# One exp for both units of a head in the last attention, and two smaller edits elsewhere, in an eight-stage decoder kernel

## The chip, the cores and the metric

The kernel runs on one core of a Trainium2 chip. The metric is the device time of one execution in microseconds. The kernel before was timed three times: 2863.63 us is the median, 2861.47 and 2869.18 us the lowest and highest.

## What is computed

The reference sends a residual stream `x` of 16 tiles of 128 rows by 256 columns through four pairs of a cross attention and a feed-forward part, each added to `x`. The change touches three of the eight stages. The stage that matters most is the last attention: 2048 queries against 2048 keys, 16 heads of 16 columns, with quantised queries, keys, values and weights.

```python
def _L3_xattn_ref(x, cond, Wq, bq, Wkv, bkv, Wp, bp):
    q = (x @ Wq + bq).reshape(1, B * N, H, hd)
    ...
    q = _fq_sym(q, axis=-1)
    k = _fq_sym(k, axis=-1)
    v = _fq_sym(v, axis=2)
    attn = jnp.einsum('bhqd,bhkd->bhqk', q, k)
    attn = jax.nn.softmax(attn.astype(jnp.float32), axis=-1)
    attn = _fq_unsigned(attn, axis=-1)
    out = jnp.einsum('bhqk,bhkd->bhqd', attn, v)
```

The second is the attention of the first feed-forward slot (`gqa`: 16 query heads and 4 key heads of 128 columns, softmax over 128 keys with a causal mask), the third the masked cross attention with the ternary feed-forward part (`mask_bit`).

## The kernel before, in words

Every stage is one block in which each engine has its own instruction list, written out by hand; semaphores tie the lists together. An engine runs its list strictly in order, so an instruction that waits holds back all that stand behind it.

**Last attention (`attend3`).** The work is cut into 512 units. A unit `u` is one tile of 128 query rows (`t = u // 32`), one head and one half of the keys: 128 x 1024 scores. Two units make a head, 32 units a tile. A unit passes through these steps:

1. `score(u)` on TensorE: two matmuls of 512 columns into one of three two-bank slots `S[:, u % 3]` of PSUM (6 of the 8 banks).
2. `maximum(u)` on VectorE: scales the scores, writes them to `kept[:, u % 4]` in SBUF and takes the row maximum. The odd unit goes on from the maximum of the even one.
3. `bias(n)` on GpSimd, once for each head: turns the maximum into exp's bias.
4. `exp(u)` on ScalarE: 128 x 1024, writes the counts `ex[:, u % 4]` as uint16 and sums them.
5. `turn(u)` on TensorE: eight transposes into the one bank `TPW`.
6. `evacuate(u)`: copies the turned bank to `pw[:, u % 4]`, on ScalarE for three units of four, on VectorE for the fourth.
7. `attend(u)` on TensorE: eight matmuls of 16 columns with the values.

TensorE's list is `score(u)`, `turn(u - 4)`, `attend(u - 5)`. At each tile's end VectorE adds up and inverts the sums (`row_steps`), and scales the output (`scale_rows`, `scale_columns`).

**Grouped attention (`gqa`).** The loop over 16 tiles is pipelined: in step `i` TensorE turns and scores tile `i`, then does the queries and values of tile `i + 2`, then `turn_p(i)`, `attend(i)`, `project(i)`. In the last two steps (`i` = 14 and 15) there is no tile `i + 2`. `exp(t)` has four groups of four heads; `sums(t)` on VectorE waits for all four, inverts the 16 sums and multiplies 128 x 2048 at once; `turn_p(t)` waits for that, turns four groups of four heads, and `turned_p(t)` copies them on ScalarE.

**Masked attention (`mask_bit`).** Eight pairs of tiles. TensorE's step `i` begins with `scores(i)`, right behind the `turn_x(i)` that ends step `i - 1` and that ScalarE copies (`turned_x`) before the scores can begin. `keep_busy(nc, k, bank, n)` issues `n` matmuls of 512 columns whose results nobody reads; there is one such call in each step, before `turn_b`.

Of the kernel before, what the change touches and what calls it, by code (L numbers as in the profile page):

```python
# [16 lines left out]
P = 128  # L17
# [663 lines left out]
def gqa(nc, k, x_in, hid_out, arena, load_next, hand):  # L681
# [8 lines left out]
    with ExitStack() as ctx:  # L690
# [116 lines left out]
        def _(act):  # L807
# [29 lines left out]
            def exp(t):  # L837
                for b in range(4):
# [5 lines left out]
            def turned_p(t):  # L844
                for g in range(PG):
# [9 lines left out]
            for i in range(-2, B):  # L855
# [4 lines left out]
                at(exp, i)  # L860
                at(queries, i + 2)
                at(values, i + 2)
                at(turned_p, i)
# [3 lines left out]
        def _(dve):  # L867
# [68 lines left out]
            def sums(t):  # L936
                dve.wait_ge(s["exped"], t * 4 + 4)
                nc.vector.reciprocal(mx[:, 2], mx[:, 1]).then_inc(s["row_recip"], 1)
                dve.wait_ge(s["row_recip"], t + 1)
                nc.vector.tensor_tensor(pr[:], pr[:], mx[:, 2].unsqueeze(2).to_broadcast([P, GH, P]), ALU.mult).then_inc(s["p_norm"], 1)  # L940
# [17 lines left out]
        def _(pe):  # L958
# [1629 lines left out]
def attend3(nc, k, qT_in, steps, out, KT, V, v_step, load_next, hand, qt):  # L2588
# [8 lines left out]
    LAG = 4  # L2597
    LN255 = 5.541263545158426
    with ExitStack() as ctx:
        def sb(name, shape, dt=F32):  # L2600
# [4 lines left out]
            zeroed scores kept bias exped turned evacuated  # L2605
            attended both row_recip probs_step scaled o_done""")
# [7 lines left out]
        sums = sb("sums", [P, 2, 2, NH])  # L2614
        tot = sb("tot", [P, 2, 3, NH])
# [5 lines left out]
        block = ctx.enter_context(nc.Block())  # L2621

# [121 lines left out]
        def _(pe):  # L2744
# [33 lines left out]
            for u in range(NU + LAG + 1):  # L2778
                if u < NU:
                    score(u)  # L2780
# [630 lines left out]
```

## Time and profile before

| | |
|---|---|
| median of three runs | 2863.63 us |
| the profiled execution, its own time | 2859.6 us |
| its span, first to last instruction | 2857.8 us |
| mean granted TensorE clock | 0.964 |
| busy: TensorE, VectorE, ScalarE, GpSimd | 85%, 67%, 59%, 20% |
| last attention | about 1660 to 2498 us of the span |
| grouped attention | about 190 to 697 us |
| masked attention | about 970 to 1150 us |

The shares of busy time are means over stages with different limits: what a stage is bound by has to be read inside it. A duration in the timeline runs from an instruction's start to its end, and the next one often starts some 0.1 us before that end, so what an instruction costs its engine is the distance between two starts.

### The profile page before, as it was taken

What the parts mean: (1) busy time and instruction counts of PE and PEld (TensorE: products, weight loads), DVE (VectorE), ACT (ScalarE), POOL (GpSimd) and SP (SyncE); (2) the same over time, 40 slices, a digit from 0 to 9 for tenths busy, and PEclk for the clock granted to TensorE, in tenths of its full rate; (3) what the DMA queues carried; (4) which work ended last, traced back from release to release, by engine and by line L of the source; (5) the groups of instructions that cost most, each with busy time, mean ns of one, the idle gap of its engine ahead of it and who ended that gap; (6) DMA issues with size and microseconds to landing.
All of it is one profiled execution on the core that took longest, in us unless ns stands there. A gap on an engine that the chain in (4) does not pass through costs nothing. (4 is left out here: it accounts for less than half of the span.)

```text
span 2857.8 us, 52551 instructions
## 1 busy us (share of the span) xinstructions
PE 2421.5 (85%) x19942; PEld 1626.7 (57%) x19942; DVE 1910.8 (67%) x4532; ACT 1689.4 (59%) x3423; POOL 581.8 (20%) x658
## 2 busy tenths in 40 slices
PE   6978999997999786788897777777777777799999
PEld 5745766665666543566565544444444444456666
DVE  6856666663344288675776889999999999833231
ACT  4536676764333266344443489999999999823222
POOL 2214434340221133321221310000000000021211
PEclk9989999999999889999999999999999999999999
DMA  3120000002010210211002220000000000000000
GB/s 142 41 82 8 8 12 16 8 5 80 15 34 8 77 57 15 77 38 43 21 25 85 89 100 16 9 15 11 9 24 9 9 17 9 7 24 23 19 4 12
DMA packets 58953, 92.93 MB, mean 33 GB/s; under 512 B 5440, under 2 KB 54608, under 8 KB 57680
## 3 DMA queue, kind: packets, MB, share of 16 engines
q1 hardware_dynamic: 58704, 89.57, 9.4%
q8 instruction: 161, 2.64, 0.4%
q14 instruction: 88, 0.72, 0.1%
HBM read 66.48 MB, written 23.07 MB: 31 GB/s over the span
## 5 line engine op out<-in xcount | busy, mean ns | idle before, releaser
L2671 ACT ACTIVATE attend_ex<-attend_kept,attend_mx 128x1024 uint16<-128x1024 f32 x512 | 588.1, 1153 | 2.6 <-POOL attend_mx L2656 2.6
L2764 PEld LDWEIGHTS psum<-ident_b,attend_ex 128*128 128x128 bf16 x4096 | 241.7, 98 | 424.2 <-ACT attend_ex L2671 332.1
L2764 PE MATMUL psum<-ident_b,attend_ex 128*128 128x128 bf16 x4096 | 316.5, 221 | 186.2 <-ACT attend_pw L2676 87.9
L2697 DVE CUSTOM_DVE_ANT_0 attend_kept<-psum,attend_zero,attend_mx 128x1024 f32<-128x1024 f32 x256 | 343.8, 1343 | 65.4 <-PE psum L2755 62.3
L1502 PE MATMUL psum<-arena,moe_tokT 128*128 128x512 f32 (+2 forms) x896 | 359.4, 546 | 3.0 <-DVE moe_h L1389 2.9
L2697 DVE CUSTOM_DVE_ANT_0 attend_kept<-psum,attend_zero,queries_step 128x1024 f32<-128x1024 f32 x256 | 327.5, 1279 | 11.9 <-PE psum L2755 9.3
L2755 PE MATMUL psum<-keys_turned,queries_ahead 96*128 96x512 bf16 x1024 | 308.2, 383 | 3.1 <-PEq L2271 2.0
L2676 ACT COPY attend_pw<-psum 128x512 f32<-128x512 f32 x384 | 222.6, 580 | 51.7 <-PE psum L2764 51.5
L1389 DVE TENSOR_TENSOR moe_h<-moe_sg,psum 128x512 f32<-128x512 f32 (+1 forms) x112 | 69.9, 625 | 263.9 <-PE psum L1502 256.7
L1502 PEld LDWEIGHTS psum<-arena,moe_tokT 128*128 128x128 f32 x896 | 165.2, 191 | 138.3 <-issue 119.3
L1236 ACT ACTIVATE moe_sg<-psum 128x512 f32<-128x512 f32 (+1 forms) x112 | 61.4, 548 | 290.3 <-PE psum L1502 286.0
L2656 POOL TENSOR_SCALAR attend_mx<-attend_mx 128x1 f32<-128x1 f32 x256 | 50.8, 199 | 779.0 <-DVE attend_mx L2697 779.0
L2774 PE MATMUL psum<-values,attend_pw 128*128 128x16 f16 x4096 | 178.9, 170 | 3.5 <-DVE stored_rows L2719 2.9
L1524 PE MATMUL psum<-arena,moe_hT 128*128 128x256 f32 (+1 forms) x800 | 178.9, 380 | 2.7 <-ACT moe_hT L1248 1.6
L1194 POOL TENSOR_TENSOR moe_h<-moe_h,moe_cw 128x1408 f32<-128x1408 f32 (+1 forms) x32 | 90.6, 2832 | 374.6 <-DVE moe_h L1389 367.3
L1524 PEld LDWEIGHTS psum<-arena,moe_hT 128*128 128x128 f32 (+1 forms) x800 | 150.8, 190 | 28.2 <-issue 3.3
L2774 PEld LDWEIGHTS psum<-values,attend_pw 128*128 128x128 f16 x4096 | 157.4, 97 | 5.8 <-issue 5.1
L793 POOL TENSOR_TENSOR gqa_nq<-gqa_nq,neg_half 128x20 f32<-128x20 f32 x16 | 88.2, 5511 | 148.5 <-DVE gqa_nq L911 148.5
L1246 ACT COPY moe_hT<-psum 128x512 f32<-128x512 f32 (+1 forms) x112 | 54.1, 527 | 108.7 <-PE psum L1514 108.7
L989 PE MATMUL psum<-arena,gqa_hT 128*128 128x512 f32 x256 | 113.6, 597 | 0.0
L1039 PE MATMUL psum<-arena,gqa_oT 128*128 128x256 f32 x512 | 113.1, 379 | 0.0
L1039 PEld LDWEIGHTS psum<-arena,gqa_oT 128*128 128x128 f32 x512 | 97.3, 190 | 20.1 <-issue 7.7
(454 smaller groups left out, 4732.3 us busy)
## 6 DMA issues: line engine op xcount, KB each, us to landing
residual<-stored_rows SPq DMA_DIRECT2D x48, 128.0 KB, 1.7
queries_turned<-queries_rows SPq DMA_DIRECT2D x16, 384.0 KB, 3.2
queries_ahead<-queries_turned SPq DMA_DIRECT2D x16, 384.0 KB, 3.3
arena<-in_moe SPq DMA_DIRECT2D x1, 5704.0 KB, 18.1
arena<-in_gqa SPq DMA_DIRECT2D x1, 5440.0 KB, 17.8
arena<-in_moe SPq DMA_DIRECT2D x1, 4360.0 KB, 13.2
xatt_ct<-in_ctx_T SPq DMA_DIRECT2D x32, 128.0 KB, 2.2
residual<-stored_rows SPq DMA_DIRECT2D x16, 256.0 KB, 2.1
```

Of the source, the lines that this page charges most:

```text
L793: nc.gpsimd.tensor_tensor(nq[:, j, 1], nq[:, j, 0], k["neg_half"][:].to_broadcast([P, HQK]), ALU.pow).then_inc(s["q_rms"], 1)
L989: last = nc.tensor.matmul(BIG[:, b], hT[:, ic], wq[:, ic, b * 512:(b + 1) * 512], start=ic == 0, stop=ic == DC - 1)
L1039: last = nc.tensor.matmul(Y, oT[:, c], wo[:, c], start=c == 0, stop=c == GH - 1)
L1194: nc.gpsimd.tensor_tensor(hv, hv, cw[:, i % 2, j].unsqueeze(2).to_broadcast([P, SETS, I]), ALU.mult).then_inc(s["h_done"], 1)
L1502: last = nc.tensor.matmul(bank[:, q % 2, 0:size], tokT[:, i % 2, j, ic], wt[:, ic, at:at + size], start=ic == 0, stop=ic == DC - 1)
L1524: last = nc.tensor.matmul(YB[:, j * D:(j + 1) * D], hT[0:size, j, c], wd[0:size, c], start=c == 0, stop=c == DN - 1)
L2671: nc.scalar.activation(ex[:, u % 4], kept[:, u % 4], ACT.Exp, bias=mx[:, t % 2, h, 2:3], accum_out=sums[:, t % 2, u % 2, h:h + 1]).then_in ...
L2676: nc.scalar.copy(pw[:, u % 4], TPW).then_inc(s["evacuated"], 1)
L2697: nc.vector.tensor_tensor_reduce(kept[:, u % 4], S[:, u % 3], zero[:].to_broadcast([P, UK]), steps[:, 0, t, h:h + 1], best[:, 0:1] if half ...
L2755: last = nc.tensor.matmul(S[:, u % 3, b * 512:(b + 1) * 512], qt[:, t % 2, h * P:(h + 1) * P], KT[:, c:c + 4, h // 2], start=True, stop=True)
L2764: last = nc.tensor.transpose(TP[:, c], counts[u % 4][:, c * P:(c + 1) * P], k["ident_b"][:])
L2774: last = nc.tensor.matmul(O[:, h * HD:(h + 1) * HD], pT[u % 4][:, c], V[:, kc, h * HD:(h + 1) * HD], start=kc == 0, stop=kc == B - 1)
```

## The change

Three edits.

In `attend3` the two exps of a head become one over 128 x 2048. To keep both units of a head next to each other for longer, `kept` has eight slots instead of four and moves into the weight arena that the stage does not use. The scores have two PSUM slots instead of three, and the two banks set free give the turned counts three banks instead of one. ScalarE copies 15 of 16 turned banks, VectorE the sixteenth (before 3 of 4 and 1 of 4). TensorE issues five units of scores first, and then `turn(u)`, `score(u + 5)`, `attend(u - 2)`. The two partial sums are one, so that an add in `row_steps` goes.

In `gqa` VectorE normalises each group of four heads as soon as its exps are done, and TensorE turns it on its own. In the last two tiles ScalarE puts the first group's copy ahead of the fourth group's exps.

In `mask_bit` four filler matmuls stand ahead of the scores of pairs 1 to 7.

```diff
 # attend3
-        S = k["psum"][:, 0:6, :].rearrange("p (u b) c -> p u (b c)", b=2)
-        TPW = k["psum"][:, 6, :]
-        TP = TPW.bitcast(BF16).rearrange("p (c m) -> p c m", m=P)
+        S = k["psum"][:, 0:4, :].rearrange("p (u b) c -> p u (b c)", b=2)
+        TPW = k["psum"][:, 4:7, :]
+        TP = TPW.rearrange("p r c -> p (r c)").bitcast(BF16).rearrange("p (r c m) -> p r c m", r=TR, m=P)
-        kept = sb("kept", [P, 4, UK])
+        kept = arena[:, 0:KR * UK].rearrange("p (r c) -> p r c", r=KR)
...
+        def on_dve(u):
+            return u % DR == DR - 1
...
-            def exp(u):
-                t, h = u // UN, u % UN // 2
-                if u % 2 == 0:
-                    act.wait_ge(s["bias"], u // 2 + 1)
-                if u >= 4:
-                    act.wait_ge(s["turned"], u - 3)
-                nc.scalar.activation(ex[:, u % 4], kept[:, u % 4], ACT.Exp, bias=mx[:, t % 2, h, 2:3],
-                                     accum_out=sums[:, t % 2, u % 2, h:h + 1]).then_inc(s["exped"], 1)
+            def exp(n):
+                t, h, u = n // NH, n % NH, 2 * n
+                act.wait_ge(s["bias"], n + 1)
+                if n >= 2:
+                    act.wait_ge(s["turned"], u - 2)
+                nc.scalar.activation(ex[:, u % 4:u % 4 + 2], kept[:, u % KR:u % KR + 2], ACT.Exp, bias=mx[:, t % 2, h, 2:3],
+                                     accum_out=sums[:, t % 2, h:h + 1]).then_inc(s["exped"], 2)
...
-            for u in range(0, NU, 2):
-                exp(u)
-                if u % 4 == 2:
-                    evacuate(u - 1)
-                exp(u + 1)
-                evacuate(u)
+            for n in range(NU // 2 + 1):
+                if n < NU // 2:
+                    exp(n)
+                for u in range(2 * n - 2, 2 * n):
+                    if u >= 0 and not on_dve(u):
+                        evacuate(u)
...
-                if u >= 4:
-                    dve.wait_ge(s["exped"], u - 3)
+                if u >= KR:
+                    dve.wait_ge(s["exped"], u - KR + 1)
...
-            for u in range(NU + LAG + 1):
+            for u in range(5):
+                score(u)
+            for u in range(NU + 2):
                 if u < NU:
-                    score(u)
-                if LAG <= u < NU + LAG:
-                    turn(u - LAG)
-                if u > LAG:
-                    attend(u - LAG - 1)
+                    turn(u)
+                if u + 5 < NU:
+                    score(u + 5)
+                if u >= 2:
+                    attend(u - 2)
 # gqa: ScalarE, VectorE, TensorE
+                else:
+                    exp(i, range(0, 3))
+                    turned_p(i, range(0, 1))
+                    exp(i, range(3, 4))
+                    turned_p(i, range(1, PG))
...
-                dve.wait_ge(s["exped"], t * 4 + 4)
-                nc.vector.reciprocal(mx[:, 2], mx[:, 1]).then_inc(s["row_recip"], 1)
+                for b in range(4):
+                    heads = slice(4 * b, 4 * b + 4)
+                    dve.wait_ge(s["exped"], t * 4 + b + 1)
...
-                pe.wait_ge(s["p_norm"], t + 1)
                 for g in range(PG):
                     n = t * GROUPS + QG + g
+                    pe.wait_ge(s["p_norm"], t * 4 + g + 1)
 # mask_bit, TensorE
             for i in range(NI + 2):
+                if 1 <= i < NI:
+                    keep_busy(nc, k, 6, 4)
                 at(scores, i)
```

On ScalarE in the last attention, before, from inside the first tile: `attend_ex<-attend_kept` is an exp, `attend_pw<-psum` the copy of a turned bank.

```order
L2676 COPY attend_pw<-psum 128x512
L2671 ACTIVATE attend_ex,attend_sums<-attend_kept,attend_mx 128x1024
L2676 COPY attend_pw<-psum 128x512
L2671 ACTIVATE attend_ex,attend_sums<-attend_kept,attend_mx 128x1024
L2676 COPY attend_pw<-psum 128x512
L2671 ACTIVATE attend_ex,attend_sums<-attend_kept,attend_mx 128x1024 x2
```

And now, around the first turned bank that VectorE takes (`arena` is where `kept` lies):

```order
L2690 COPY attend_pw<-psum 128x512 x2
L2685 ACTIVATE attend_ex,attend_sums<-arena,attend_mx 128x2048
L2690 COPY attend_pw<-psum 128x512 x2
L2685 ACTIVATE attend_ex,attend_sums<-arena,attend_mx 128x2048
L2690 COPY attend_pw<-psum 128x512
L2685 ACTIVATE attend_ex,attend_sums<-arena,attend_mx 128x2048
L2690 COPY attend_pw<-psum 128x512 x2
```

Each exp covers a head; two copies stand between two exps, or one.

On TensorE, from the start of the same stage, before: `ident_b` marks the turning, `values` the attending, `keys_turned` the scoring.

```order
L2755 MATMUL psum<-keys_turned,queries_ahead 128x512 x10
L2764 MATMUL psum<-ident_b,attend_ex 128x128 x8
L2755 MATMUL psum<-keys_turned,queries_ahead 128x512 x2
L2764 MATMUL psum<-ident_b,attend_ex 128x128 x8
L2774 MATMUL psum<-values,attend_pw 128x16 x8
L2755 MATMUL psum<-keys_turned,queries_ahead 128x512 x2
L2764 MATMUL psum<-ident_b,attend_ex 128x128 x8
L2774 MATMUL psum<-values,attend_pw 128x16 x8
```

And now:

```order
L2767 MATMUL psum<-keys_turned,queries_ahead 128x512 x10
L2776 MATMUL psum<-ident_b,attend_ex 128x128 x8
L2767 MATMUL psum<-keys_turned,queries_ahead 128x512 x2
L2776 MATMUL psum<-ident_b,attend_ex 128x128 x8
L2767 MATMUL psum<-keys_turned,queries_ahead 128x512 x2
L2776 MATMUL psum<-ident_b,attend_ex 128x128 x8
L2767 MATMUL psum<-keys_turned,queries_ahead 128x512 x2
L2786 MATMUL psum<-values,attend_pw 128x16 x8
L2776 MATMUL psum<-ident_b,attend_ex 128x128 x8
L2767 MATMUL psum<-keys_turned,queries_ahead 128x512 x2
```

In the steady part the scores now stand behind the turning and are for a unit five ahead, and the attending is for a unit two behind; there are as many matmuls as before.

On ScalarE at the end of the grouped attention, before: `gqa_pr` is an exp (16 heads), `gqa_pT` the copy of a turned group, `gqa_oT` a copy of the attended heads.

```order
L848 COPY gqa_pT<-psum 128x512 x4
L853 COPY gqa_oT<-psum 128x512 x4
L835 COPY gqa_qkT<-psum 128x512 x5
L841 ACTIVATE gqa_pr,gqa_mx<-gqa_pr,gqa_mx 128x128 x16
L848 COPY gqa_pT<-psum 128x512 x4
L853 COPY gqa_oT<-psum 128x512 x4
```

And now, in the last two tiles:

```order
L853 COPY gqa_oT<-psum 128x512 x4
L835 COPY gqa_qkT<-psum 128x512 x5
L841 ACTIVATE gqa_pr,gqa_mx<-gqa_pr,gqa_mx 128x128 x12
L848 COPY gqa_pT<-psum 128x512
L841 ACTIVATE gqa_pr,gqa_mx<-gqa_pr,gqa_mx 128x128 x4
L848 COPY gqa_pT<-psum 128x512 x3
L853 COPY gqa_oT<-psum 128x512 x4
```

The copy of the first turned group has moved in front of the last four exps.

## Rows read from the trace of the kernel before

**Rows 1.** The page's costliest groups: busy us, mean ns | idle before, releaser.
```profile
L2676 ACT COPY attend_pw<-psum 128x512 f32<-128x512 f32 x384 | 222.6, 580 | 51.7 <-PE psum L2764 51.5
```

**Rows 2.** Busy us by stretch: PE, PEld, DVE, ACT, POOL, then PEclk, DMA.
```profile
1660.00:2498.00 838.00, 646.22 (x9215) 404.26 (x9213) 759.23 (x1232) 780.44 (x1409) 50.84 (x256) 0.98 0.06 19
```

**Rows 3.** ScalarE's timeline in the last attention: start us, us, engine, line.
```profile
1999.55 1.16 ACT L2671 ACTIVATE attend_ex<-attend_kept,attend_mx 128x1024 uint16<-128x1024 f32 x1
...
2000.69 0.58 ACT L2676 COPY attend_pw<-psum 128x512 f32<-128x512 f32 x1
2001.16 1.16 ACT L2671 ACTIVATE attend_ex<-attend_kept,attend_mx 128x1024 uint16<-128x1024 f32 x1
...
2002.30 1.14 ACT L2671 ACTIVATE attend_ex<-attend_kept,attend_mx 128x1024 uint16<-128x1024 f32 x1
...
2003.82 0.59 ACT L2676 COPY attend_pw<-psum 128x512 f32<-128x512 f32 x1 [0.28 <-PE psum L2764]
2004.31 1.15 ACT L2671 ACTIVATE attend_ex<-attend_kept,attend_mx 128x1024 uint16<-128x1024 f32 x1
...
2005.91 1.16 ACT L2671 ACTIVATE attend_ex<-attend_kept,attend_mx 128x1024 uint16<-128x1024 f32 x1
```

**Rows 4.** Three source lines: duration ns min/median/max, first and last start.
```profile
L2671 ACT ACTIVATE attend_ex<-attend_kept,attend_mx x512: 1132/1152/1164, 1663.4 to 2492.8; 128x1024 uint16<-128x1024 f32 x171
...
L1259 ACT ACTIVATE ternary_weights<-arena,minus_magic x3: 1985/1985/1993, 884.1 to 945.5; 128x2048 bf16<-128x2048 f32 x3
...
L2969 ACT ACTIVATE mbit_hq<-mbit_ag,minus_magic x16: 1132/1140/1152, 1014.4 to 1142.6; 128x1024 bf16<-128x1024 f32 x16
```

**Rows 5.** TensorE's timeline, same stretch: turning, attending, scoring of a unit.
```profile
2001.41 0.61 PE L2764 MATMUL psum<-ident_b,attend_ex 128*128 128x128 bf16 x8 [0.38 <-ACT attend_pw L2676]
...
2001.86 0.35 PE L2774 MATMUL psum<-values,attend_pw 128*128 128x16 f16 x8
...
2002.06 0.59 PE L2755 MATMUL psum<-keys_turned,queries_ahead 96*128 96x512 bf16 x2
```

**Rows 6.** TensorE's timeline at the stage's start, clock at the lower level.
```profile
1664.71 1.04 PE L2764 MATMUL psum<-ident_b,attend_ex 128*128 128x128 bf16 x8 [0.52 <-ACT attend_ex L2671]
...
1665.54 1.06 PE L2755 MATMUL psum<-keys_turned,queries_ahead 96*128 96x512 bf16 x2
```

**Rows 7.** VectorE's timeline at the start of the last attention.
```profile
1660.31 1.28 DVE L2697 CUSTOM_DVE_ANT_0 attend_kept<-psum,attend_zero,queries_step 128x1024 f32<-128x1024 f32 x1 [5.99 <-PE psum L2755]
...
1661.75 1.34 DVE L2697 CUSTOM_DVE_ANT_0 attend_kept<-psum,attend_zero,attend_mx 128x1024 f32<-128x1024 f32 x1
...
1663.02 1.28 DVE L2697 CUSTOM_DVE_ANT_0 attend_kept<-psum,attend_zero,queries_step 128x1024 f32<-128x1024 f32 x1
```

**Rows 8.** Timeline of the next-to-last tile of the grouped attention.
```profile
652.26 0.25 DVE L938 RECIPROCAL gqa_mx<-gqa_mx 128x16 f32<-128x16 f32 x1 [3.22 <-ACT gqa_pr L841]
652.55 2.29 DVE L940 TENSOR_TENSOR gqa_pr<-gqa_pr,gqa_mx 128x2048 f32<-128x2048 f32 x1
...
654.89 3.52 PE L1019 MATMUL psum<-ident,gqa_pr 128*128 128x128 f32 x16 [6.82 <-DVE gqa_pr L940]
...
658.25 3.60 PE L1030 MATMUL psum<-gqa_pT,gqa_v 128*128 128x512 f32 x8
```

**Rows 9.** Busy us by stretch, masked attention: five engines, PEclk, DMA.
```profile
1045.00:1065.00 20.00, 16.79 (x90) 9.98 (x89) 17.00 (x52) 12.68 (x24) 6.75 (x5) 0.83 0.15 52
1065.00:1084.00 19.00, 14.84 (x90) 8.20 (x88) 17.46 (x55) 13.04 (x25) 6.75 (x5) 1.00 0.10 29
```

**Rows 10.** TensorE's timeline, masked attention: turn_x, then scores.
```profile
1046.37 0.66 PE L3144 MATMUL psum<-ident,mbit_xn 128*128 128x128 f32 x4
...
1066.26 0.66 PE L3144 MATMUL psum<-ident,mbit_xn 128*128 128x128 f32 x4
...
1084.61 0.66 PE L3144 MATMUL psum<-ident,mbit_xn 128*128 128x128 f32 x4
1086.25 0.68 PE L3180 MATMUL psum<-mbit_ct,mbit_xT 128*128 128x128 f32 x4 [0.98 <-issue]
```

More of the change, by code:

```diff
@@ L835, in turned_qk, with exp @@
                     nc.scalar.copy(qkT[:, 4 * KF[g]:4 * KF[g] + 4], TP[:, n % 2]).then_inc(s["evacuated"], 1)
-            def exp(t):
-                for b in range(4):
+            def exp(t, groups):
+                for b in groups:
                     act.wait_ge(s["shifted"], t * 4 + b + 1)
@@ L842, in exp, with turned_p @@
                     last.then_inc(s["exped"], 1)
-            def turned_p(t):
-                for g in range(PG):
+            def turned_p(t, groups):
+                for g in groups:
                     n = t * GROUPS + QG + g
@@ L859, in _ @@
                 at(lambda t: turned_qk(t, range(2, QG)), i)
[L860 to L863, printed above, removed]
+                if i + 2 < B:
+                    at(lambda t: exp(t, range(4)), i)
+                    at(queries, i + 2)
+                    at(values, i + 2)
+                    at(lambda t: turned_p(t, range(PG)), i)
+                else:
[3 more added lines that the diff above has]
+                    turned_p(i, range(1, PG))
                 at(attended, i)
@@ L2585, in _, with attend3 @@
                 at(turn_x, i + 2)
-def attend3(nc, k, qT_in, steps, out, KT, V, v_step, load_next, hand, qt):
+def attend3(nc, k, qT_in, steps, out, KT, V, v_step, arena, load_next, hand, qt):
     W3 = 3 * 32
@@ L2596, in attend3 @@
     NU = B * UN
-    LAG = 4
+    KR, TR, DR = 8, 3, 16
     LN255 = 5.541263545158426
@@ L2694, in maximum @@
                     dve.wait_ge(s["kept"], u)
[L2695 to L2697 removed]
+                if u >= KR:
+                    dve.wait_ge(s["exped"], u - KR + 1)
+                nc.vector.tensor_tensor_reduce(kept[:, u % KR], S[:, u % 2], zero[:].to_broadcast([P, UK]), steps[:, 0, t, h:h + 1], best[:, 0:1] if half else -3.0e38,
                                                ALU.add, ALU.max, best[:, half:half + 1]).then_inc(s["kept"], 1)
@@ L2724, in scale_columns @@
                 nc.vector.tensor_tensor(o[:, t % 2], o[:, t % 2], v_step[:], ALU.mult).then_inc(s["o_done"], 1)
-            for u in range(0, NU, 2):
+            for u in range(NU + 5):
                 t, at = u // UN, u % UN
-                maximum(u)
-                if t and at == LAG:
-                    scale_rows(t - 1)
-                maximum(u + 1)
-                if u % 4 == 2 and u >= 4:
-                    evacuate(u - 3)
-                if t and at == 2:
-                    row_steps(t - 1)
-                if t and at == LAG:
-                    scale_columns(t - 1)
+                if u < NU:
+                    maximum(u)
+                if u >= 5 and on_dve(u - 5):
+                    evacuate(u - 5)
+                if t and u < NU:
+                    if at == 4:
+                        row_steps(t - 1)
+                    if at == 6:
+                        scale_rows(t - 1)
+                    if at == 7:
+                        scale_columns(t - 1)
             row_steps(B - 1)
-            evacuate(NU - 1)
             scale_rows(B - 1)
@@ L3319, in build @@
             qkv3(nc, k, res[0], ctx_T, qT, steps, KT, V, v_step, arena[0], nothing, hand(6, 8, 10), q_rows, q_ahead)
-            attend3(nc, k, qT, steps, att, KT, V, v_step, loader("moe3", W_MOE3, 1), hand(7, 10, 12, x0, (1, att)), q_ahead)
+            attend3(nc, k, qT, steps, att, KT, V, v_step, arena[0], loader("moe3", W_MOE3, 1), hand(7, 10, 12, x0, (1, att)), q_ahead)
         moe(nc, k, W_MOE3, res[0], att, out, arena[1], nothing, hand(8, 12, 14))
```

42 lines of the change are left out of this document (21 added, 21 removed).

## The prediction, made before the changed kernel ran

> **What bounds the kernel now.** I read the windows first, to find the stages, then the page's groups, the timeline of the largest stage, and the timeline at the two smaller places. The last attention is 838 us of 2857.8, and in it ScalarE is busy for 780 us, VectorE for 759, TensorE for 646 at a granted clock of 0.98 of 2.4 GHz [rows 2]. No engine is full, so the stage is a loop in which two nearly full engines also wait for each other. The reader is to see where in [rows 3]: four exps and three copies of ScalarE take from 1999.55 to 2005.91, that is 6.36 us for four units or 3.18 for a head. Distances between starts give what each costs: exp then exp 1.14 (2001.16 to 2002.30), exp plus copy 1.61, a copy between 0.47 (2000.69 to 2001.16) and 0.49 (2003.82 to 2004.31). Four exps and three copies are 4 x 1.14 + 3 x 0.475 = 5.98; the other 0.38 is the stall ahead of the copy at 2003.82, of which the row shows 0.28. Over the stage ScalarE's copies waited 51.7 us for turned banks [rows 1]. The stall comes from the single turned bank: the turning at 2001.41 began only when a copy had emptied the bank [rows 5], and the unit that VectorE copies empties it late. From the first exp (1663.4) to the end of the last one (2492.8 + 1.14) it is 830.5 us for 256 heads, 3.24 us each, the ends of tiles included [rows 4].
>
> **The last attention.** *The exps.* 512 exps of 1024 columns become 256 of 2048. No exp of 2048 columns is in the trace. The nearest rows are one kind of ScalarE instruction with a bias from SBUF in two lengths: 1.140 us for 1024 columns, 1.985 for 2048 [rows 4], so 1024 more columns cost 0.845 us. The exp of 1024 takes 1.152, near the first. I take 1.14 + 0.845 = 1.99 us from start to start for the new exp, against 2.28 for the two: 0.29 less per head, 75 us over the stage. The bounds: 1.95 (the columns alone cost 2 x 0.845 = 1.69, and something fixed is sure to stay), and 2.28, where merging saves nothing; I take 1.99, since the long row is of the same form.
>
> A rule of the Trainium skill prices this lower. "ScalarE: Activation LUTs", section "What ACT_TABLE_LOAD costs", gives an instruction with a bias operand some 280 ns beside its columns, of which 93 ns overlap with its neighbour; that is an estimate of 187 ns per exp saved, 48 us in all, and the total below would be 2801 us. The page does not count the read of the accumulated sum that goes with each exp here; the distances between starts do, so my sum goes by them.
>
> *The copies.* ScalarE takes on 15 of 16 units instead of 3 of 4: 480 copies instead of 384. With 0.49 each (two copies now stand together, so I take the dearer one), the steady cost of a head is 1.99 + 2 x 0.49 = 2.97, and in one head of eight, where VectorE takes a copy, 2.48. The mean is 2.91. With 0.47 it would be 2.87, which is 10 us less over the stage.
>
> *The stall.* Whether ScalarE then runs without gaps depends on two suppliers. TensorE: per unit it turns in 0.45 (2001.41 to 2001.86), attends in 0.20, and scores in at most 0.59 [rows 5], 2.48 per head, under 2.91. With three turned banks `turn(2n)` and `turn(2n + 1)` go as soon as exp `n` is done, while ScalarE copies the two units before for 0.98 us and then runs the next exp for 1.99; the turned banks are ready 1 us before they are asked for. VectorE: the even maximum costs 1.44 (1660.31 to 1661.75, the odd one waits for its result) and the odd 1.27 (1661.75 to 1663.02) [rows 7], 2.71 per head. Copies fall from one unit in four to one in sixteen, and the end of a tile adds some 1.2 us; that makes about 2.83 per head, under 2.91 but close.
>
> What is queued behind the new waits: `score(u + 5)` stands behind `turn(u)`, which waits for exp, so VectorE's supply comes in bursts of two after each exp. From the end of exp `n`, `score(2n + 5)` is done after some 0.1 + 0.45 + 0.6 = 1.15 us, the odd maximum 1.35 later, GpSimd's bias 0.4 later: 2.9 us. Exp `n + 2`, which needs it, cannot start before 0.98 + 1.99 + 0.98 = 3.95. So 1 us is spare and absorbs the ends of tiles, which cost about 1.2 but lie partly in VectorE's own wait of 0.17 between an even and an odd maximum. I allow 0.2 us a tile, 3 us, and 4 us for the fill (the second exp waits for its two maxima) and for what a transfer or a clock dip disturbs.
>
> *Sum.* 256 x 2.91 = 745, plus 7, is 752, against 830.5. The fill before the first exp and the drain after the last keep their form. **The stage gives 78 to 80 us; I take 79.**
>
> **The grouped attention.** In steps 0 to 13 TensorE has queries and values ahead of `turn_p` and does not wait for the normalised rows; the four shorter multiplications lie under that work, as the one long did: 0. If that cover were gone, 14 tiles times about 0.4 us more VectorE work would be 6 us. In steps 14 and 15 nothing covers it: TensorE stands 6.82 us until the multiplication of 2.29 us is done, begins to turn at 654.89 and to attend at 658.25 [rows 8]. Now groups 0 to 2 are turned while the later exps run. ScalarE's one copy in front of the last four exps delays these by a wait for the bank and 0.49, about 1.1 us; they end at 653.2 instead of 652.1. Then come 0.2 for the inversion, a quarter of the multiplication (0.65 with its fixed part), and one group of transposes (3.52 / 4 = 0.9): attending begins at about 655.3, 2.9 us earlier. Twice, **6 us**; bounds 3 and 7.
>
> **The masked attention.** Steps at the full clock take 18.35 us (1066.26 to 1084.61), those with the clock at 0.83 on average 19.9 (1046.37 to 1066.26) [rows 9, 10]; four steps of the latter kind, which is what fits between the stage's filling and 1066, would give back 4 x 1.54 = 6 us at most if the clock stayed at 2.4 GHz. The four fillers cost 4 x 0.21 = 0.85 us at 2.4 GHz, between `turn_x` and the scores, where TensorE waits 0.98 for ScalarE's copy [rows 10]: they cost nothing there, and at 1.2 GHz (1.7 us) some 0.75 each, 3 us for four steps. They raise TensorE's activity just ahead of the stretch in which the clock falls. I take half, **3 us** gained; bounds 6 gained and 3 lost.
>
> **The sum** against the profiled execution's 2859.6 us: 2859.6 - 79 - 6 - 3 = 2771.6. The median of the runs shown is 4.0 us above that execution, so the median to expect is **2775 us**.
>
> **The rivals.**
>
> *A, as forecast:* 2775, own range 2755 to 2795 (the copy's price 10 us down, an exp of 2.05 us 15 up, the two small edits 10 either way). For it: with these prices ScalarE needs 2.91 us per head, VectorE 2.83 and TensorE 2.48, and the exps have 1 us to spare. Chance 0.78.
>
> *B, VectorE and TensorE hand over too slowly:* with two score slots instead of three, `score(u + 5)` waits for `maximum(u + 3)`, and a maximum finds its scores late if TensorE is in a turning at that moment. Each maximum covers 1.27 us; a wait of 0.1, a turning and attending of 0.65 and scores of 0.6 are 1.35. If that 0.1 and the full wait behind exp showed in every head, the period would be 2.83 + 0.25 = 3.08, the stage 795 us, and the time 2818. Against it: on average TensorE has 0.43 us or more to spare. Chance 0.13.
>
> *C, the long exp saves nothing:* 2.28 + 0.94 = 3.22 per head, no gain in the stage beyond 6 us: 2849. Both rows of [rows 4] speak against it. Chance 0.03.
>
> *D, slower, the clock:* TensorE's idle time, now cut in two pieces per head, gathers in one piece before each exp's end. At the lower level turning takes 0.83 and scoring 1.06 [rows 6], attending twice 0.20: 2.29 per unit, 4.58 per head, and TensorE would be the bound. A share f of the stage at that level gives 2.91 (1 - f) + 4.58 f per head; it decides from f = 0.2 on, where 3.24 is reached, and with the whole stage at the lower level the time is 3200. Against it: TensorE's work per microsecond grows, and the stage runs at 0.98 now [rows 2]. Chance 0.06: 0.03 for slower, 0.02 for a share of the stage that just eats the gain, 0.01 for less. "TensorE: Matmul & The Clock Gate", section "A second HAM failure mode: psum-queue depth-cycling", speaks for this rival: short idles between groups of matmuls can make the clock swing. By that rule the time would be D's.
>
> **The numbers.** The likeliest is 2775. The range 2752 to 2810 takes in A with a little to spare and the nearer half of B, 0.8 in all. A measurement of this kernel tells about 0.3%, 9 us, from no change. Faster: A, B, C and 0.01 of D, 0.95; within 0.3%: 0.02 of D; slower: 0.03 of D.
>
> **What would show it.** Right: the exp of 2048 lasts about 2.0 us and is followed by two copies 0.49 apart; starts of exps are 2.97 apart; ScalarE's idle before the copies falls from 51.7 us to under 10; TensorE's wait is for exp, not for a copy; the stage takes about 759 us. In the grouped attention the wait ahead of the first turning in the last two tiles is shorter and attending begins 3 us earlier. In the masked one PEclk reads 1.00 in pairs 2 to 4. Wrong: an idle in front of the exps that GpSimd's bias ends (B), an exp of over 2.1 us (C), PEclk under 0.9 in the stage (D), or VectorE's maxima getting longer beside longer reads by ScalarE.

## The result and the profile after

| | before | changed |
|---|---|---|
| median (lowest to highest, 4 runs each) | 2864.11 us (2861.47 to 2869.18) | 2770.99 us (2764.47 to 2773.87) |
| ratio, 95% interval | | 0.967 (0.9647 to 0.9693) |
| the profiled execution, its span | 2859.6, 2857.8 us | 2773.2, 2771.3 us |
| mean granted clock | 0.964 | 0.97 |

The change saves 93 us. The forecast was 2775 us, range 2752 to 2810: the measured time lies in it, 4 us below the forecast. Of the kernels tried below, three had one execution that took clearly longer than their others: 5883.35 us (`gqa` alone) and 3404.26 us (two exps a head), which their medians and ratios leave out, and 2808.56 us (VectorE copies every 4th), which stays in, pulls that ratio up and widens its interval.

**The last attention.** The window over the stage, and then the page's groups of its three engines, beside [rows 2] and [rows 1]:

```profile
1657.60:2410.40 752.80, 605.43 (x9216) 449.51 (x9216) 687.26 (x1120) 743.89 (x993) 50.55 (x257) 0.99 0.06 21
```
```profile
L2685 ACT ACTIVATE attend_ex<-arena,attend_mx 128x2048 uint16<-128x2048 f32 x256 | 535.3, 2091 | 1.6 <-PE psum L2776 1.0
L2776 PE MATMUL psum<-ident_b,attend_ex 128*128 128x128 bf16 x4096 | 316.9, 220 | 128.5 <-ACT attend_ex L2685 123.9
L2711 DVE CUSTOM_DVE_ANT_0 arena<-psum,attend_zero,attend_mx 128x1024 f32<-128x1024 f32 x256 | 343.7, 1342 | 57.4 <-PE psum L2767 43.8
L2711 DVE CUSTOM_DVE_ANT_0 arena<-psum,attend_zero,queries_step 128x1024 f32<-128x1024 f32 x256 | 327.5, 1279 | 6.3 <-PE psum L2767 6.3
...
L2690 ACT COPY attend_pw<-psum 128x512 f32<-128x512 f32 x480 | 278.0, 667 | 1.0 <-PE psum L2776 1.0
```

The window is 752.8 us instead of 838, and ScalarE is busy for 99% of it. Its idle time before the copies is 1.0 us instead of 51.7. The waits have moved to the others: TensorE waits 123.9 us for exps before it turns, VectorE 50 us for scores, and neither costs anything as long as ScalarE has work. The window starts 2 us before the one of before and its clock is as high (0.99 against 0.98).

The timeline of ScalarE over two heads (start, duration):

```profile
2000.56 2.02 ACT L2685 ACTIVATE attend_ex<-arena,attend_mx 128x2048 uint16<-128x2048 f32 x1
2002.47 0.21 ACT L2685 ACTIVATION_READ_ACCUMULATOR attend_ex<-arena,attend_mx 128x1 f32 x1
2002.56 1.08 ACT L2690 COPY attend_pw<-psum 128x512 f32<-128x512 f32 x2
2003.50 2.04 ACT L2685 ACTIVATE attend_ex<-arena,attend_mx 128x2048 uint16<-128x2048 f32 x1
2005.40 0.23 ACT L2685 ACTIVATION_READ_ACCUMULATOR attend_ex<-arena,attend_mx 128x1 f32 x1
2005.50 1.10 ACT L2690 COPY attend_pw<-psum 128x512 f32<-128x512 f32 x2
2006.44 2.05 ACT L2685 ACTIVATE attend_ex<-arena,attend_mx 128x2048 uint16<-128x2048 f32 x1
```

From start to start an exp costs 2.00 us and two copies cost 0.94, so 0.47 each; a head takes 2.94. And TensorE's timeline in the same stretch, beside [rows 5]:

```profile
2002.73 0.62 PE L2776 MATMUL psum<-ident_b,attend_ex 128*128 128x128 bf16 x8 [0.53 <-ACT attend_ex L2685]
2003.19 0.60 PE L2767 MATMUL psum<-keys_turned,queries_ahead 96*128 96x512 bf16 x2
2003.63 0.35 PE L2786 MATMUL psum<-values,attend_pw 128*128 128x16 f16 x8
2003.83 0.61 PE L2776 MATMUL psum<-ident_b,attend_ex 128*128 128x128 bf16 x8
```

The turning starts 0.17 us after the copies do: it waits for the exp, and no longer for a copy to empty the bank. It is ready at 2003.19, and its own copy starts at 2005.50, 2.3 us later. The second turning of the head is ready at 2004.44, 1.5 us before its copy.

**The grouped attention.** TensorE, then VectorE's last inversion and multiplication, then two copies of turned groups on ScalarE, in the next-to-last tile, beside [rows 8]:

```profile
652.86 0.66 PE L1027 MATMUL psum<-ident,gqa_pr 128*128 128x128 f32 x4 [1.84 <-DVE gqa_pr L948]
653.68 0.66 PE L1027 MATMUL psum<-ident,gqa_pr 128*128 128x128 f32 x4 [0.16 <-DVE gqa_pr L948]
654.63 0.66 PE L1027 MATMUL psum<-ident,gqa_pr 128*128 128x128 f32 x4 [0.30 <-DVE gqa_pr L948]
656.67 1.12 PE L1027 MATMUL psum<-ident,gqa_pr 128*128 128x128 f32 x4 [1.38 <-ACT gqa_pT L848]
657.58 1.92 PE L1038 MATMUL psum<-gqa_pT,gqa_v 128*128 128x512 f32 x2
```
```profile
655.71 0.18 DVE L946 RECIPROCAL gqa_mx<-gqa_mx 128x4 f32<-128x4 f32 x1 [1.14 <-ACT gqa_pr L841]
655.93 0.69 DVE L948 TENSOR_TENSOR gqa_pr<-gqa_pr,gqa_mx 128x512 f32<-128x512 f32 x1
```
```profile
655.59 1.05 ACT L848 COPY gqa_pT<-psum 128x512 f32<-128x512 f32 x2
```

Three groups are turned while the last exps run. This tile begins on TensorE at 644.58 and attends 13.00 us later; before it began at 641.63 and attended 16.62 us later. The 1.38 us before the fourth turning are put down to a copy on ScalarE, and here the label misleads. The turned groups share two banks, so the fourth turning needs the second group's copy, which is the first of the two in the last row: it started at 655.59 and took 0.56 us, and was done at 656.15. The multiplication of the fourth group ended at 656.62 (655.93 and 0.69), and the turning started 0.05 us behind it, as each turning before did behind its own multiplication. So the multiplication ends the wait; the copy that the label names is the third group's, which ended close by. The attending itself then took 4.67 us instead of 3.44 (it ran at a granted clock of 0.74, before at 1.00), so 2.4 of the 3.6 us stay in this tile.

**The masked attention.** The starts of three steps on TensorE, beside [rows 10], with the fillers of the new kind behind them:

```profile
1039.80 0.66 PE L3158 MATMUL psum<-ident,mbit_xn 128*128 128x128 f32 x4
1040.29 1.03 PE L166 MATMUL psum<-ident_b 128*128 128x512 bf16 x4
...
1058.15 0.66 PE L3158 MATMUL psum<-ident,mbit_xn 128*128 128x128 f32 x4
...
1076.50 0.66 PE L3158 MATMUL psum<-ident,mbit_xn 128*128 128x128 f32 x4
```
```profile
1039.80:1058.15 18.35, 15.42 (x92) 8.52 (x93) 16.89 (x51) 12.46 (x25) 6.74 (x5) 1.00 0.17 58
```

The steps are 18.35 us each at a granted clock of 1.00, which is 2.4 GHz; in the profile of the kernel before they took 19.9 at 0.83 in this place. That is not all the fillers' doing: see the fillers alone, below.

### The profile page after: what moved, and what is told of

Its sections match the earlier page's. It is cut to its first block and busy times, and to the rows that moved or that the text cites. A ratio compares the mean times of both kernels' runs of the same rounds, so it can differ in the third digit from the quotient of the medians.

```text
span 2771.3 us, 52221 instructions
## 1 busy us (share of the span) xinstructions
PE 2384.0 (86%) x19970; PEld 1670.0 (60%) x19970; DVE 1848.9 (67%) x4516; ACT 1650.5 (60%) x3007; POOL 581.3 (21%) x658
## 5 line engine op out<-in xcount | busy, mean ns | idle before, releaser
L2685 ACT ACTIVATE attend_ex<-arena,attend_mx 128x2048 uint16<-128x2048 f32 x256 | 535.3, 2091 | 1.6 <-PE psum L2776 1.0
L2776 PE MATMUL psum<-ident_b,attend_ex 128*128 128x128 bf16 x4096 | 316.9, 220 | 128.5 <-ACT attend_ex L2685 123.9
L2711 DVE CUSTOM_DVE_ANT_0 arena<-psum,attend_zero,attend_mx 128x1024 f32<-128x1024 f32 x256 | 343.7, 1342 | 57.4 <-PE psum L2767 43.8
L2711 DVE CUSTOM_DVE_ANT_0 arena<-psum,attend_zero,queries_step 128x1024 f32<-128x1024 f32 x256 | 327.5, 1279 | 6.3 <-PE psum L2767 6.3
L2776 PEld LDWEIGHTS psum<-ident_b,attend_ex 128*128 128x128 bf16 x4096 | 234.0, 98 | 152.4 <-ACT attend_ex L2685 151.2
L2690 ACT COPY attend_pw<-psum 128x512 f32<-128x512 f32 x480 | 278.0, 667 | 1.0 <-PE psum L2776 1.0
L2786 PEld LDWEIGHTS psum<-values,attend_pw 128*128 128x128 f16 x4096 | 176.0, 96 | 141.9 <-issue 24.5
```

What stands on the lines that cost most here:

```text
L2685: nc.scalar.activation(ex[:, u % 4:u % 4 + 2], kept[:, u % KR:u % KR + 2], ACT.Exp, bias=mx[:, t % 2, h, 2:3], accum_out=sums[:, t % 2, h: ...
L2690: nc.scalar.copy(pw[:, u % 4], TPW[:, u % TR]).then_inc(s["by_act"], 1)
L2711: nc.vector.tensor_tensor_reduce(kept[:, u % KR], S[:, u % 2], zero[:].to_broadcast([P, UK]), steps[:, 0, t, h:h + 1], best[:, 0:1] if hal ...
L2776: last = nc.tensor.transpose(TP[:, u % TR, c], counts[u % 4][:, c * P:(c + 1) * P], k["ident_b"][:])
L2786: last = nc.tensor.matmul(O[:, h * HD:(h + 1) * HD], pT[u % 4][:, c], V[:, kc, h * HD:(h + 1) * HD], start=kc == 0, stop=kc == B - 1)
```

## Experiments

The parts of the change apart, then single sizes. "Last attention" is the distance from the first exp to the last in the profile of each kernel, so the unchanged stages are not in it.

| kernel | median us | ratio to before, 95% | last attention |
|---|---|---|---|
| before | 2864.11 | | 829.4 |
| changed | 2770.99 | 0.967 (0.9647 to 0.9693) | 741.5 |
| `attend3` alone | 2779.25 | 0.9701 (0.9685 to 0.9718) | 740.8 |
| `gqa` alone | 2859.14 | 0.9982 (0.9974 to 0.9991) | 830.0 |
| fillers alone | 2861.76 | 0.999 (0.9982 to 0.9998) | 829.5 |
| changed, two exps a head | 2831.54 | 0.9883 (0.9867 to 0.99) | 808.6 |
| changed, two turned banks | 2778.87 | 0.9695 (0.9681 to 0.971) | 751.2 |
| changed, scores four ahead | 2892.14 | 1.0093 (1.0078 to 1.0108) | 867.8 |
| changed, VectorE copies every 4th | 2781.88 | 0.9738 (0.969 to 0.9787) | 754.5 |
| changed, every 8th | 2758.87 | 0.963 (0.9615 to 0.9646) | 729.4 |
| changed, again | 2768.18 | 0.9659 (0.9646 to 0.9672) | 740.5 |
| changed, every 8th, again | 2757.23 | 0.9619 (0.9606 to 0.9632) | 730.0 |
| changed, every 10th | 2761.13 | 0.9633 (0.9616 to 0.9649) | 729.7 |
| changed, scores six ahead | 2765.76 | 0.9642 (0.9629 to 0.9655) | 736.9 |

The ratios are to runs of the kernel before on the same chip (medians 2863.65 to 2866.63).

### The three edits alone

`attend3` of the changed kernel in the kernel before:

```diff
-            attend3(nc, k, qT, steps, att, KT, V, v_step, loader("moe3", W_MOE3, 1), hand(7, 10, 12, x0, (1, att)), q_ahead)
+            attend3(nc, k, qT, steps, att, KT, V, v_step, arena[0], loader("moe3", W_MOE3, 1), hand(7, 10, 12, x0, (1, att)), q_ahead)
```

> The kernel before with the new last attention alone. My theory: nearly all of the gain is here, since that stage went from 838.5 to 752.7 us in the two traces: 2864 - 86 = 2778 us, and 2.94 us from exp to exp. The rival, that the smaller edits or a calmer clock in other stages carry a third of the gain, would give 2800 or more.

Measured: 2779.25 us, 84.4 below the kernel before of the same comparison (2863.65).

`gqa` alone (per-group normalising, first group's copy ahead of the last exps in the last two tiles), and the fillers alone:

```diff
+                if 1 <= i < NI:
+                    keep_busy(nc, k, 6, 4)
                 at(scores, i)
```

> The kernel before with the grouped attention's edit alone. My theory: each of the last two tiles ends 2.4 us earlier and the 14 others do not gain: 2864 - 5 = 2859 us. The rival: the shorter pieces cost as much in the 14 covered tiles as they give in the last two, 2864 us.

> The kernel before with the four fillers of the masked attention alone. My theory: the fillers hold the clock at its upper level and the steps fall from 19.9 to 18.35 us: 2864 - 6 = 2858 us, and PEclk 1.00 from pair 1 on. The rival, that the clock's dips in this stage come and go by themselves: no difference to the kernel before and PEclk 0.83 in the first steps in this profile.

Measured: 2859.14 and 2861.76 us, 4.5 and 1.9 below. By the ratios the three save 85.6, 5.2 and 2.9 us (1 - ratio, times 2863.65), together 93.7; the whole change saves 93.1 by the medians, and 98.5 when it was timed again (2866.63 less 2768.18). So the three add up, to within the 5 us by which these two timings differ. Not tried apart are the two parts of the `gqa` edit and, within `attend3`, the eight slots of `kept` and the two slots of the scores.

The fillers' interval almost touches 1. In the profiles TensorE's `turn_x` runs from its first start to its last in 126.8 to 129.3 us in the kernels with fillers and in 131.2 to 133.2 in the three without. The steps tell what is theirs. The second and third take 19.1 to 19.2 and 19.5 to 19.6 us in the three kernels without fillers, and 17.2 to 17.3 and 18.3 to 18.4 in ten of the eleven with them: 3.1 us, which agrees with the 2.9 by the ratio. (The eleventh, two turned banks, has 19.1 and 18.35.) The later steps are not theirs: the 19.9 us of the fourth and fifth are in the profile of the kernel before alone, while `attend3` alone and `gqa` alone, which have no fillers either, take 18.36 us there at a granted clock of 1.00; and a slow step of some 19.5 us comes later in some kernels of both kinds. The fillers alone came out 4 us above their expectation, because it was taken from the one profile with two more slow steps.

### Two exps again, all else changed

```diff
-                nc.scalar.activation(ex[:, u % 4:u % 4 + 2], kept[:, u % KR:u % KR + 2], ACT.Exp, bias=mx[:, t % 2, h, 2:3],
-                                     accum_out=sums[:, t % 2, h:h + 1]).then_inc(s["exped"], 2)
+                for j in range(2):
+                    last = nc.scalar.activation(ex[:, u % 4 + j], kept[:, u % KR + j], ACT.Exp, bias=mx[:, t % 2, h, 2:3],
+                                                accum_out=sums[:, t % 2, j, h:h + 1])
+                last.then_inc(s["exped"], 2)
```

> The changed kernel with its exp split into two of 128 x 1024 again, back to back, the signal still given after the second; the add of the two sums is back. All else stays: banks, order, copies. My theory: ScalarE is the bound and each head costs 2 x 1.14 instead of 2.00, so 0.28 x 256 = 72 us more: 2843 us, starts of heads 3.22 us apart. The rival, that the gain is the removed stall and the third bank: at most 20 us more, under 2795 us.

ScalarE's timeline of this kernel:

```profile
2006.12 1.56 ACT L2686 ACTIVATE attend_ex<-arena,attend_mx 128x1024 uint16<-128x1024 f32 x1
...
2007.27 1.55 ACT L2686 ACTIVATE attend_ex<-arena,attend_mx 128x1024 uint16<-128x1024 f32 x1
...
2008.40 1.47 ACT L2692 COPY attend_pw<-psum 128x512 f32<-128x512 f32 x2
2009.34 1.57 ACT L2686 ACTIVATE attend_ex<-arena,attend_mx 128x1024 uint16<-128x1024 f32 x1
```

A head takes 3.22 us (2006.12 to 2009.34): 1.15 + 1.13 + 0.94. Against 2.94 the one exp saves 0.28. The stage is 67 us longer than with one exp (808.6 against 741.5), and the time 61 to 63 us (2831.54 less 2770.99 or 2768.18); this is the largest part of the change. Expected was more, 2843: the shorter period of the changed kernel lets the ends of tiles show (below), and the longer one hides them. The other 21 us of the stage (829.4 less 808.6) are the rest of `attend3`'s edit: before, a head took 3.18 us steadily and 3.24 in the mean; here 3.22, and 2.75 in one head of eight, 3.16 in the mean of these, and 3.35 at the end of a tile. The stalls that are gone are about paid for by the copies that ScalarE took on; what is left is mostly the ends of tiles.

### Two turned banks in place of three

```diff
-    KR, TR, DR = 8, 3, 16
+    KR, TR, DR = 8, 2, 16
```

> The changed kernel with two turned banks instead of three. My theory: the second bank is what removes the stall, since both units of a head are turned while the two copies before them end; the third gives nothing: 2771 us. The rival, three banks are needed: TensorE would wait for copies again, 0.1 to 0.2 us per head, 2797 to 2822 us.

It was slower, by 8 to 11 us. TensorE's timeline and ScalarE's, of the kernel with two banks:

```profile
2003.78 1.08 ACT L2690 COPY attend_pw<-psum 128x512 f32<-128x512 f32 x2
...
2004.72 2.04 ACT L2685 ACTIVATE attend_ex<-arena,attend_mx 128x2048 uint16<-128x2048 f32 x1
```
```profile
2004.52 0.61 PE L2776 MATMUL psum<-ident_b,attend_ex 128*128 128x128 bf16 x8 [0.65 <-ACT attend_pw L2690]
```

The turning starts 0.74 us behind the copies' start instead of 0.17, and it waits for a copy. In an ordinary head that costs ScalarE nothing, exps stay 2.94 apart. But the scores stand behind the turning and so come 0.6 us later too, and that shows where the slack is smallest: in the exps behind a head of which VectorE copies a unit the distances are 2.63 and then 3.07, or 3.50 at a tile's end, instead of 2.46, 2.94 and 3.22. With 31 such heads, 15 of them at a tile's end, this is 31 x 0.17 + 16 x 0.13 + 15 x 0.28 = 11.6 us, and the stage shows 9.7 to 10.7. That the third bank does nothing was wrong.

### Scores four and six units ahead

```diff
-            for u in range(5):
+            for u in range(4):
                 score(u)
...
-                if u + 5 < NU:
-                    score(u + 5)
+                if u + 4 < NU:
+                    score(u + 4)
```

> The changed kernel with scores four units ahead instead of five. My theory: the odd unit of the head after next is then scored only behind the second turning, its bias is there about 4.0 us after an exp's end, and that exp should start 3.9 us after it; ScalarE begins to wait, 0.1 to 0.15 us per head: 2795 to 2810 us. The rival, the lead does not matter since VectorE has spare time: 2771 us.

The whole gain was lost and more: 2892.14, 0.9% slower than before. The chain in the timeline of this kernel, all engines:

```profile
1998.15 2.00 ACT L2685 ACTIVATE attend_ex<-arena,attend_mx 128x2048 uint16<-128x2048 f32 x1 [0.46 <-issue]
...
2000.30 0.62 PE L2776 MATMUL psum<-ident_b,attend_ex 128*128 128x128 bf16 x8 [1.19 <-ACT attend_ex L2685]
...
2000.76 0.60 PE L2767 MATMUL psum<-keys_turned,queries_ahead 96*128 96x512 bf16 x2
...
2001.09 2.01 ACT L2685 ACTIVATE attend_ex<-arena,attend_mx 128x2048 uint16<-128x2048 f32 x1
...
2001.39 1.28 DVE L2711 CUSTOM_DVE_ANT_0 arena<-psum,attend_zero,queries_step 128x1024 f32<-128x1024 f32 x1 [0.74 <-PE psum L2767]
...
2002.82 1.34 DVE L2711 CUSTOM_DVE_ANT_0 arena<-psum,attend_zero,attend_mx 128x1024 f32<-128x1024 f32 x1
...
2004.25 0.19 POOL L2671 TENSOR_SCALAR attend_mx<-attend_mx 128x1 f32<-128x1 f32 x1 [3.33 <-DVE attend_mx L2711]
...
2004.53 2.00 ACT L2685 ACTIVATE attend_ex<-arena,attend_mx 128x2048 uint16<-128x2048 f32 x1 [0.37 <-issue]
```

Exp `n` at 1998.15, then turning, scores of the even unit of head `n + 2`, its even maximum, the odd one, the bias, and exp `n + 2` at 2004.53: 6.38 us for two heads, where ScalarE's own work is 5.88. So the loop, and no engine, is the bound, at 3.19 us a head. Five ahead only the odd unit's scores are in this chain, and it is one maximum (1.43 us) shorter: 4.95, worked out so, which leaves 0.93 us to spare. The profile of the changed kernel bears it out: in the heads furthest from a disturbance the bias is done 0.85 to 0.96 us before its exp starts. The rest of the loss is at the ends of tiles: a chain with nothing to spare passes every delay on. Exp starts repeat from tile to tile after 54.62 us (1994.63 to 2049.25) instead of 16 x 3.19 = 51.04. For a tile, the chain costs 51.04 less the 46.1 us of ScalarE's own work (14 x 2.94 and 2 x 2.46), 4.9 us, and the end of the tile 3.6 us: 16 x 4.9 and 15 x 3.6 are 132 us, and the stage is 126 us longer than in the changed kernel, whose ends of tiles also cost some 4. The expectation had 25 to 40 us: it took the chain's excess at a third to a half of its size, and did not have the ends of tiles.

> Scores six units ahead instead of five, everything else as changed. Main theory, an exp has about 1 us to spare at five: no change, 2771 us (2767 to 2775). Rival 1, the ends of tiles still cost ScalarE something because its supply is late: 4 to 8 us less. Rival 2, TensorE now waits for a maximum in front of the odd turning and the copy behind it comes late: more than 5 us more.

Measured six ahead, 2765.76 us against 2768.18 of the changed kernel in the same comparison: the medians lie 2.4 us apart and the intervals of the ratios overlap. In the profile the stage is 3.6 us shorter, mostly since the distance at a tile's end is 3.05 instead of 3.22. Five is enough, to within the 4 us that the ends of tiles still cost.

### How many units VectorE copies

```diff
-    KR, TR, DR = 8, 3, 16
+    KR, TR, DR = 8, 3, 8
```

> The changed kernel with VectorE copying one turned bank in eight instead of one in sixteen. My theory, ScalarE is the bound: 32 copies of 0.47 us leave it, 15 us, of which VectorE, now near 2.90 us per head, lets through about half: 2764 us. The rival, VectorE and the handover are the bound already: 32 copies of 0.43 to 0.6 us more, 2785 us.

> The changed kernel with VectorE copying one bank in four, the share of the kernel before. ScalarE then needs 2.00 + 1.5 x 0.47 = 2.71 us per head, VectorE 2.71 + 0.5 x (0.43 to 0.6) + 0.09 = 3.02 to 3.10. My theory: VectorE becomes the bound and the time rises by 20 to 40 us, 2791 to 2811 us. The rival, VectorE's row times overstate its cost and the handover has room: faster than 2771, down to 2750 us.

> VectorE copies every eighth unit, beside the changed kernel in the same comparison. If the earlier 2758.9 us was the kernel and not the day: 2759 (2756 to 2762), 12 us under the changed kernel. If it was drift of the clock in other stages, the distance is under 6 us.

> The changed kernel itself, timed beside the next ones. All theories: 2771 us (2768 to 2774), and the time of the stages that the change does not touch as before.

> VectorE copies every tenth unit, 51 of 512 instead of 32 (the changed kernel) or 64 (every eighth). Main theory, ScalarE is the bound and each copy taken from it gives 0.47 us less about 0.1 for the wait it makes: the time lies on a line between the two, about 2764 us. Rival, at every eighth VectorE is already the bound and the best division lies between: under 2758 us.

The windows of the last attention with every 8th unit (again) and with every 4th:

```profile
1658.00:2391.00 733.00, 605.53 (x9181) 446.54 (x9181) 697.20 (x1141) 729.48 (x960) 50.22 (x255) 0.99 0.06 18
```
```profile
1658.00:2414.00 756.00, 649.21 (x9160) 445.46 (x9158) 731.65 (x1205) 717.95 (x893) 50.70 (x255) 0.97 0.06 18
```

If ScalarE alone set the time, the stage would be 255 distances of 2.94 us, less 0.94 in the first, less 0.47 for each copy that VectorE takes between: 734.2 us with 31 (every 16th), 725.3 with 50 (10th), 719.2 with 63 (8th), 689.1 with 127 (4th). Measured are 6 to 7, 4, 10 to 11 and 65 us more. Down to every 10th unit ScalarE is the bound; at every 8th the rest of the loop eats what it still gives; at every 4th VectorE is busy for 97% of the stage and is the bound. There the exps start alternately 2.69 and 3.07 us apart, which is VectorE's own work: 1.42 and 1.27 for the two maxima, and 0.39 more for a copy, since 0.21 of the copy's 0.60 falls into the gap between the two maxima. The expectation had 0.43 to 0.6 for it and 20 to 40 us of loss; the kernel lost 11 to 14. Every 8th and every 10th are alike (the intervals overlap), and both are faster than the changed kernel: in one comparison 2757.23 and 2761.13 against 2768.18. For every 8th the intervals of the ratios are apart; for every 10th they touch (0.9649 and 0.9646), and the stage, 11 us shorter, is the better sign. The line between the ends that was expected for every 10th is not there in the stage; it is flat from 10 to 8.

## Why the prediction was right

**What bounds the stage.** Right. ScalarE is the bound after the change, full to 99%, and TensorE waits for exps, not for copies, as was named.

**The exps.** Taken 1.99 us from start to start, measured 2.00; taken saving 0.29 a head, measured 0.28. The longer instruction of the same form in another stage was a good price. The rule of the Trainium skill, "ScalarE: Activation LUTs", section "What ACT_TABLE_LOAD costs", gave an estimate of 187 ns for each exp saved, 48 us; the kernel with two exps shows 280 ns where nothing else moves, 67 us over the stage and 61 to 63 us in the time. Here the measurement decides, and it is above the page's price.

**The copies.** This is the one term that was mis-sized. The dearer of two distances, 0.49, was taken; in the new order it is 0.47. That is 480 x 0.02 = 9.6 us. The steady mean was forecast at 2.91 a head with 0.49, 2.87 with 0.47; measured are 2.94 and in one head of eight 2.46, a mean of 2.88.

**The stall and the ends of tiles.** Idle before the copies fell from 51.7 to 1.0 us. The allowance of 0.2 us a tile and 4 us for the fill was about right: in the second profile of the changed kernel the ends of tiles cost 3.23 instead of 2.94, 15 x 0.29 = 4.4 us. What they wait for is the bias, and behind it VectorE, in the same profile:

```profile
2033.20 0.69 DVE L2716 COPY attend_pw<-psum 128x512 f32<-128x512 f32 x1
2033.81 0.24 DVE L2721 RECIPROCAL attend_tot<-attend_sums 128x16 f32<-128x16 f32 x1
...
2034.24 1.34 DVE L2711 CUSTOM_DVE_ANT_0 arena<-psum,attend_zero,attend_mx 128x1024 f32<-128x1024 f32 x1
...
2035.67 0.19 POOL L2671 TENSOR_SCALAR attend_mx<-attend_mx 128x1 f32<-128x1 f32 x1 [3.31 <-DVE attend_mx L2711]
```

VectorE's one copy of the 16 units stands at the tile's end, together with the inversion of the sums, and the next exp starts at 2035.95, 0.09 us behind the bias. Banks were ready earlier than forecast, 2.3 and 1.5 us ahead and not 1. The stage, from the first exp to the end of the last, was forecast at 752 from 830.5; it is 743.5 (1662.9 to 2404.4, and 2.0) in the one profile and 742.5 in the other, 87 to 88 us instead of 79, and the 9.6 us of the copies, less 2.6 for the exp's 2.00 in place of 1.99, are about that difference.

**The grouped attention.** Forecast 6; measured 5.2 by the ratio of the edit alone. In the profiles the stage (first transpose of `gqa_h` to the first matmul that reads `moe_tokT`) takes 511.6 to 511.8 us without the edit and 503.7 to 506.2 with it, and the stage behind it, up to the first `turn_x` of the masked attention, 268.0 to 268.9 without and 269.5 to 270.3 with it, which takes a part back. The sum was right, and the path that of the forecast (last exps, inversion, a quarter of the multiplication, one group of transposes), with two sizes off: the last exps were delayed by the copy's 0.48 us (653.55 to 654.03) and not by 1.1, so attending began 3.6 and not 2.9 us earlier; and the attending was 1.2 us longer at a lower clock, which was not forecast. The two errors partly cancel, which is luck.

**The masked attention.** Forecast 3, bounds 6 and -3; measured 2.9 by the ratio of the edit alone (0.6 to 5.2 by its interval) and 3.1 by the second and third step in the profiles. PEclk reads 1.00 where it was 0.83, as named, but from the fourth step on it does so without fillers too. Half of the bound was taken without a reason for the half; that it came out is in part luck.

**The sum.** 79 + 6 + 3 = 88 was forecast, 93 measured by the medians and 98 when timed again, so that a part of the closeness of 2775 and 2771 is luck. With the larger term of the stage it would be 96 to 97. The profiles show what took some of it back: in the unchanged stage before the last attention, from the last matmul of `arrow_xT` to the first turning, the kernel before took 146.4 us and the changed kernel 151.9 and 154.4; 0.9 of that is the first exp, which is longer now. But the kernels with `gqa` or the fillers alone take 148.9 and 149.9 there, so the profile of before has this stretch unusually fast; its granted clock was 1.00 from 1533 to 1593 and 0.89 in the changed kernel. Why the clock differs there was not tried, nor why the stage behind the grouped attention is longer in every kernel with that edit.

**The rivals.** B, a slow handover between TensorE and VectorE, did not come with five units ahead, and it is what four units ahead shows: there VectorE does wait for scores (0.74 us at 2001.39), but not as the short waits that repeat of which B was made; it is a closed chain through exp, which costs nothing until it is longer than ScalarE's own work for two heads, and then everything. C fell with the exp of 2.00 us. D, the clock, did not come: 0.99 in the stage. The rule of "TensorE: Matmul & The Clock Gate", section "A second HAM failure mode: psum-queue depth-cycling", in the Trainium skill spoke for it; here TensorE has an idle of some 0.5 us before each head's turning over 740 us, and the clock stayed at the upper level.

## What to carry to other kernels

Price a longer instruction by the distance between starts of the same form elsewhere in the trace, and when an engine is at its bound, move small work to its neighbour until the neighbour is as full: VectorE at every 8th to 10th unit gave another 0.25 to 0.4%. When the order of a loop is changed, count the time once around it (here exp, turning, scores, two maxima, bias, exp) against the work of the bounding engine over the same number of heads: one unit less ahead put a maximum more into the chain and cost 121 us, one more brought at most a few. A buffer can hold slack where no wait shows on the path: what the third turned bank removes costs nothing in an ordinary head, and it was worth 8 to 11 us at the heads that are shorter or stand at a tile's end. And when an instruction waits for two things, check the label of the wait against the ends of both: the fourth turning of the grouped attention was labelled with a copy and waited for a multiplication.

## What the runs showed of the hardware

The recorded durations of ScalarE's instructions grow while their cost does not. Timeline of the changed kernel, second profile, around a tile's end, and then the groups of exps in the changed kernel and in the one with six units ahead (duration in ns, lowest, median, highest):

```profile
2030.26 2.19 ACT L2685 ACTIVATE attend_ex<-arena,attend_mx 128x2048 uint16<-128x2048 f32 x1
2032.16 0.38 ACT L2685 ACTIVATION_READ_ACCUMULATOR attend_ex<-arena,attend_mx 128x1 f32 x1
2032.25 0.76 ACT L2690 COPY attend_pw<-psum 128x512 f32<-128x512 f32 x1
2032.72 2.19 ACT L2685 ACTIVATE attend_ex<-arena,attend_mx 128x2048 uint16<-128x2048 f32 x1
...
2034.72 1.25 ACT L2690 COPY attend_pw<-psum 128x512 f32<-128x512 f32 x2
2035.95 2.00 ACT L2685 ACTIVATE attend_ex<-arena,attend_mx 128x2048 uint16<-128x2048 f32 x1
```
```profile
L2685 ACT ACTIVATE attend_ex<-arena,attend_mx x256: 1985/2087/2197, 1662.9 to 2404.4; 128x2048 uint16<-128x2048 f32 x128
```
```profile
L2685 ACT ACTIVATE attend_ex<-arena,attend_mx x256: 1985/3084/3152, 1662.1 to 2399.0; 128x2048 uint16<-128x2048 f32 x128
```

The exp of 2.19 us starts its successor after 2.46 with a copy of 0.47 between, so it costs 2.00 all the same; after the wait at the tile's end (2032.72 to 2035.95 is 3.23) the record is 2.00 again. With six units ahead, where ScalarE waits least, the median record is 3.08 us, longer than the 2.94 between starts, and the stage is shorter. So on an engine that never waits, a record's duration, and a mean or busy time made of it, is no price; the distance between starts is. Idle time suffers too: the 15 ends of tiles cost 4.4 us, but the record before each is so long that the profile counts no idle there, and only 1.1 us before exps in the whole stage of the second profile. Why the records grow was not tried.
